# A transformer block on one core: the loops over the attention heads are replaced by instructions written out for every head

## The reference

```
q, k, v = x @ wq.T, x @ wk.T, x @ wv.T      # per head, [1024, 128]
q, k = rope(rmsnorm(q)), rope(rmsnorm(k))
s = 50 * tanh(q @ k.T * scale / 50)         # causal
x = layernorm(x + softmax(s) @ v @ wo.T)
x = layernorm(x + moe(x) + shared_ffn(x))   # 32 experts, 6 of them per token
```

## Time and profile before

| | us |
|---|---|
| median of 3 runs | 1119.45 |
| lowest, highest | 1116.04, 1123.36 |
| the profiled execution | 1122.51 |
| its span, first to last instruction | 1120.8 |
| PE busy in the span | 1038.1 |
| DVE busy | 831.9 |
| ACT busy | 699.9 |
| POOL busy | 631.6 |

### The profile page before, as it was taken

The page is one execution under the profiler, slowest core; times in us unless marked ns, Lnnn a source line. Parts: engine busy times, 40 slices in busy tenths (PEclk is TensorE's granted clock), DMA queues, the critical chain, the costliest instruction groups (busy, mean ns, idle before and its releaser), DMA issues.

```text
span 1120.8 us, 20581 instructions
## 1 busy us (share of the span) xinstructions
PE 1038.1 (93%) x6304; PEld 831.9 (74%) x6304; DVE 831.9 (74%) x1360; ACT 699.9 (62%) x1159; POOL 631.6 (56%) x668
## 2 busy tenths in 40 slices
PE   4688999999999999999999999999999959989766
PEld 3567888888888888888888888888888746445432
DVE  3377888888888888888888898988898775713203
ACT  3465777777777777777777777777777632322212
POOL 0265666666666666666666666666666652363332
PEclk9899999999999999999999999999999887989977
DMA  9100000000011010101000000000000009539427
GB/s 331 31 29 30 29 29 28 28 28 28 28 33 40 30 38 20 37 24 33 25 32 28 28 28 28 28 28 28 28 28 20 20 3 294 138 96 268 74 29 229
DMA packets 47195, 65.99 MB, mean 59 GB/s; under 512 B 7904, under 2 KB 38592, under 8 KB 47168
## 3 DMA queue, kind: packets, MB, share of 16 engines
q1 hardware_dynamic: 43376, 60.65, 17.6%
q0 software_dynamic: 3072, 4.46, 2.2%
q10 hardware_dynamic: 720, 0.54, 0.2%
HBM read 54.35 MB, written 11.29 MB: 59 GB/s over the span
## 4 chain that ended last, share of the span: by engine, by line
PE 78%; DMA 11%; DVE 5%; issue 2%; POOL 2%; ACT 1%; SPq 1%; ACTq 0%; POOLq 0%; DVEq 0%
PE ps L387 20%; PE ps L388 19%; PE ps L389 19%; PE ps L415 9%; DMA acc_rows<-ye,acci 7%; PE ps L421 4%; PE ps L559 2%; PE ps L603 2%; DMA qsq<-rq_rows 1%; DMA yacc<-in_x 1%; DVE prob_lo L1057 1%; POOL pacc L933 1%; PE ps L569 1%; DVE qhat_lo L1057 1%; POOL xg L1013 1%
## 5 line engine op out<-in xcount | busy, mean ns | idle before, releaser
L1057 DVE TENSOR_TENSOR prob_lo<-praw,prob_hi 128x1024 fp32r<-128x1024 f32 (+7 forms) x256 | 313.2, 1251 | 3.2 <-ACT prob_hi L718 3.2
L916 POOL TENSOR_SCALAR_AFFINE_SELECT praw<-praw 128x128 f32<-128x128 f32 x256 | 119.6, 469 | 307.0 <-ACT praw L765 288.4
L933 POOL TENSOR_TENSOR pacc<-pacc,praw 128x768 f32<-128x768 f32 (+2 forms) x192 | 241.8, 1259 | 16.6
L759 ACT ACTIVATE praw<-ps,rk 128x1024 f32<-128x1024 f32 (+7 forms) x256 | 186.0, 740 | 88.3 <-PE ps L389 78.5
L718 ACT ACTIVATE prob_hi<-praw 128x1024 fp32r<-128x1024 f32 (+7 forms) x256 | 168.0, 683 | 1.1 <-POOL praw L916 1.1
L765 ACT ACTIVATE praw<-praw 128x1024 f32<-128x1024 f32 (+7 forms) x256 | 167.4, 681 | 0.0
L387 PE MATMUL ps<-qhat_hi,kT_hi 128*128 128x512 f32 (+3 forms) x384 | 136.4, 355 | 13.4 <-DVE qhat_lo L1057 12.9
L387 PE MATMUL ps<-prob_hi,vS_hi 128*128 128x512 f32 (+3 forms) x384 | 136.1, 354 | 4.0 <-DVE prob_lo L1057 4.0
L389 PE MATMUL ps<-qhat_hi,kT_lo 128*128 128x512 f32 (+3 forms) x384 | 133.9, 349 | 0.0
L388 PE MATMUL ps<-qhat_lo,kT_hi 128*128 128x512 f32 (+3 forms) x384 | 133.9, 349 | 0.0
L388 PE MATMUL ps<-prob_lo,vS_hi 128*128 128x512 f32 (+3 forms) x384 | 133.3, 347 | 0.0
(11 more groups left out here) (155 smaller groups left out, 1961.1 us busy)
## 6 DMA issues: line engine op xcount, KB each, us to landing
qsq<-rq_rows SPq DMA_DIRECT2D x32, 512.0 KB, 3.7
wgu<-in_wgu SPq DMA_DIRECT2D x16, 704.0 KB
wd<-in_wd SPq DMA_DIRECT2D x16, 352.0 KB
wraw<-in_wqkv SPq DMA_DIRECT2D x16, 256.0 KB, 3.7
acc_rows<-pacc SPq DMA_DIRECT2D x8, 512.0 KB, 10.9
wv<-in_wqkv SPq DMA_DIRECT2D x16, 128.0 KB, 2.1
woraw<-in_wo SPq DMA_DIRECT2D x16, 128.0 KB, 2.0
yacc<-in_x SPq DMA_DIRECT2D x1, 2048.0 KB, 14.0
```

The costliest lines, as they stand in the source:

```text
L759: nc.scalar.activation(praw[:, raw_at(b, j)], buf[:, P * j:T], ACT.Tanh, scale=rk[:, b, j:j + 1]).then_inc(tanh_done, 1)
L916: nc.gpsimd.affine_select(out=diag, in_=diag, compare_op=ALU.is_ge, fill=0.0, base=0, pattern=[[1, P]], channel_multiplier=-1).then_inc(ma ...
L933: nc.gpsimd.tensor_tensor(pacc[:, P * j:T], before, raw, ALU.add).then_inc(pacc_done, 1)
L1057: v.tensor_tensor(dst, x_, hi.bitcast(F32), ALU.subtract).then_inc(done, 1)
```

## The change

The five hardware loops become Python loops over the same bodies. The order of the instructions of each engine stays; h is now a plain number, so that the counts waited for and the DRAM addresses are constants in the instructions, and the register instructions and the branches have nothing left to do. The bodies stand 14 times (SP: 15 times) in the program instead of once.

```
-            with sp.Fori(0, H - 1) as h:
+            for h in range(0, H - 1):
...
-            with pe.Fori(1, H - 1) as h:
+            for h in range(1, H - 1):
                 for b in range(B):
                     step(Head(h, "middle"), b)
...
-            with act.Fori(1, H - 1) as h:
+            for h in range(1, H - 1):
...
-            with pool.Fori(1, H - 1) as h:
+            for h in range(1, H - 1):
...
-            with dve.Fori(1, H - 1) as h:
+            for h in range(1, H - 1):
```

## The result

The kernel after takes 1128.27 us in the median of 20 runs (1119.78 to 1137.96), the kernel before, beside it, 1121.36 us (20 runs, 1116.04 to 1128.55). The ratio is 1.0055 with a 95% interval of 1.0031 to 1.0079: half a per cent slower, within the 1% that the prediction called no change, and 7 us where it forecast 4. Two of the 20 runs (1136.71 and 1137.96 us), over 1.5% above the fastest, count as slow and are left out of the ratio; the median of the other 18 is 1127.1 us.

The account below looks back on a forecast made before the run. The prediction took PE's own matmul stream to bound the loop. Gain 0, direct stalls 0 and collisions 5 x about 1 us, rounded down to +4, gave 1119.45 + 4 = 1123 us (+0.3%), range 1114 to 1134 us.

Parts of the forecast that it names:

- Gain of the removed instructions: Register instructions and branches in the loops: covered by PE's queued work or other engines' idle time, so worth 0.
- the upper bound: PE's 210 register instructions waiting for `values` (6.7 us) plus 14 branches (3.0 us): at most 9.7 us if uncovered.
- Step 30 of before: Already written out with constants, yet its sums came 53.92 us after step 28's, the loop's round: evidence for 0 gain.
- Packets: Instruction fetches after the change: about 51 packets on q8 and some 43 on q14, spread over the span.
- Direct stalls: Engines waiting for their own instruction fetches: taken as 0; other end of the range 37 x 1.6 = 59 us.
- Place of the collision: A fetch starting in the 3.7 us between issue and landing of the query norms' broadcast can delay it.
- the 1.2 us: Delay of the query norms' broadcast per collision with a 16 KB packet, from 5.1 - 3.9 us.
- The slow step of before: Step with the broadcast at 87 us, landing in 5.1 us, the only one of three shown beside a q8 packet.
- Number of collisions: 16 KB fetches meeting the broadcast: 14% of 37, so 5; the 8 KB packets were given 0.
- the 1.3 us of slack: Time between qhat_lo's late end and PE's use of it; said to absorb 8 KB packets' 0.6 us nearly everywhere.
- Price of one: DVE's splits pushed beside POOL's accumulation: 1.8 us with output weights, 0 to 1 us without, mean about 1 us.
- the first rival: Slower: each of 5 collisions costs PE a whole late start of 5.2 us, +26 us, 1145 us; chance 0.17.

Follow-up runs that it names:

- regs_stream: Kernel before with loops and register waits kept, but as 2 rounds of 7 heads (SP 3 of 5), so bodies are long; median 1126.96 us, ratio 1.0065.
- pe_only: Kernel after with the loops of SP, ACT, POOL and DVE put back, so only PE's loop is written out; median 1123.35 us, ratio to before 1.0033.
- others_only: Kernel before with SP, ACT, POOL and DVE written out and PE's loop kept; median 1123.69 us, ratio 1.0042.
- four_delays_light: four_delays with POOL's accumulation cut to 16 columns per tile after step 0; one run, 1107.85 us.
- after_again: The kernel after, unchanged, run once more for a second profile; one run, 1122.08 us.
- four_delays: Kernel before with SP alone written out and one more small waited-for write by SP in steps 9, 14, 19 and 24; one run, 1136.45 us.

## Why the prediction held, point by point

**Gain of the removed instructions: 0, as predicted.** Between 100 and 860 us no register instruction and no branch is left on PE, and a step without a slow trip takes the 26.96 us it took in the loop. Here are SP's loop line (L335) and PE's wait of `values` (L448), the latter beside the 210 ALU_OP of the earlier trace rows, first before:

```profile
L335 SPq FUSED_REGOPS  x15: 41/41/50, 33.5 to 793.3; - x15
L335 SPq ALU_OP  x15: 37/37/37, 87.7 to 847.0; - x15
L335 SPq COMPARE_BRANCH  x15: 40/45/50, 87.8 to 847.1; - x15
...
L448 PEldq FUSED_REGOPS  x14: 55/60/60, 95.3 to 799.4; - x14
L448 PEldq EVENT_SEMAPHORE  x4: 51/51/51, 55.0 to 898.3; - x4
```

In after L335 has no instruction, and L448 has this alone:

```profile
L448 PEldq EVENT_SEMAPHORE  x32: 51/51/51, 53.7 to 902.7; - x32
```

So in before the steps written out waited with one semaphore instruction each, and those of the loop with register instructions. Over all engines, after has 2522 ALU_OP, 497 FUSED_REGOPS, 52 MOVE and 71 COMPARE_BRANCH fewer and 560 EVENT_SEMAPHORE more, which is the whole difference of 20581 and 17999. On PE's sequencer 906 of those that went stood between 100 and 860 us and took 32.6 us together, more than the 9.7 us that the prediction took for the upper bound from two kinds of them; no step got shorter by any of it. SP issues wraw 0.39 us after the broadcast instead of 0.87. Step 30 of before had told the 0, and regs_stream, as slow with its registers, does not speak against it.

**Packets: right.** 50 on q8 and 41 on q14, where 51 and 43 were worked out. From 161 to 860 us it is 36 and 28, where before had none. That q8 is PE's shows in pe_only (50 there, 13 on q14) and in others_only (14 and 41). The other engines' packets are of 8 KB (0.34 MB in 41). PE's own stream ran on beside its packets (26 of 28 steps of pe_only stayed at 26.96 us); what shows in the steps is a small DMA with a packet beside it, with trips of up to 4.28 us in after instead of 2.2.

**Direct stalls: 0 for PE's straight code, as predicted.** pe_only shows it. The one branch that did hold PE up is regs_stream's, with 3.98 us on the sequencer and a 16 KB packet in that time; before's 14 branches took at most 0.25 us, with no packet from 161 to 860 us. For DVE, step 4 of others_only leaves the question open.

**Place of the collision: wrong in the main.** The step that failed is "a fetch that starts in the 3.7 us between a broadcast's issue and landing can touch it". Of after's seven long steps only 10 and 16 have it: their broadcasts landed in 4.4 us with a 16 KB packet and in 5.2 us with an 8 KB packet beside them. The median went from 3.7 to 3.8 us, the maximum from 5.1 to 5.2. What got slower in the other five is the write ahead of it, 2.2 us long, small and waited for: +0.7 to +1.0 us beside an 8 KB packet, up to +2.3 beside a 16 KB one. The prediction left this write out. The slow step of before, from which the 1.2 us were read the earlier trace rows, had such a trip too (2.91 us).

**Number of collisions: near, by luck.** 5 were forecast, by PE's packets alone; in after seven steps are long. Only three of them (10, 20 and 25, the last with an 8 KB packet as well) have a PE packet, 4.3 us together where the prediction has 5. The other four (9, 13, 16 and 24) are q14's, 2.9 us together, and to these it gave 0: "the 1.3 us of slack holds that nearly everywhere". It doesn't: others_only, with PE's loop kept, has 3.8 us of excess. This 0 is the term that was mis-sized.

**Price of one: right in its mechanism and in its mean, wrong in its form.** The prediction named POOL's accumulation and the row that would be contended, and four_delays_light shows that nearly all of it goes with the accumulation (step 9: 35.14 us with it, 27.61 with it cut). Its "about 1 us" stands against 7.6 us over seven long steps, 1.1 each. But the price isn't one number. Counted from the profiles, over steps 3 to 30: no split beside POOL, 0 to 1.0 us (step 16 of regs_stream, with its branch, apart); wo_lo, +1.4 to 1.9; qhat_lo, +1.7 to 2.4; qhat_hi and qhat_lo in a step without weights, +5.3; all four splits, +6.2 and +8.2. So the first rival ("a whole late start", 5.2 us) was not a rival: it is the upper part of the same staircase, and pe_only reaches it in both of its collisions. The 5.2 us of step 2 of before, from which it was read, are such a case: qhat_hi and qhat_lo take 2.62 and 2.71 us there. Steps of the kind without weights were priced at 0 to 1 us; step 20 is one of them and cost 2.0.

**The sum.** +4 forecast, for the median; +7 measured, 6.0 and 7.6 us of it in the loop of two profiles. The wide spread of after's runs (18 us, before 12) fits a price that jumps with a few tenths of a us, but no run of after above 1131.04 us was profiled, so this is argued and not shown.

**Open.** Why one 16 KB packet delays the trip and another that starts at the same offset doesn't: packets that began 1.79, 1.91, 2.06 and 2.37 us into it did, others at 1.84, 1.88, 1.92, 1.93, 1.99 and 2.02 us did not. The one at 2.37 us (step 25 of pe_only) began when a regular trip is over, so it can't be its own transfer that first held that trip up. What ties long trips to fetches is that they come with streaming and at the same steps; how a fetch holds a small write up was not seen. Which of the 16 DMA engines carried a fetch was not seen either: the profile counts the packets of q8 and q14 and those of the broadcast's q1 in shares of the same 16 (0.3, 0.1 and 8.9% from 161 to 860 us), and no more.

## What to carry to other kernels

This kernel's loop had no instruction packet from 161 to 860 us; written out it had 64. Before writing such a loop out, ask not only whether the engines have cover but which small, waited-for DMA in every round has none: here 7 of 28 steps were 0.3 to 2.0 us longer, five of them with a late write of the norms. A longer loop body was no way out here: regs_stream had 55 and 57 packets too, and paid 1.4 us for PE's branch back besides. A delay was priced here by what it pushed a short instruction into: look for DVE work that ends just before a long POOL instruction starts (qhat_lo at 180.64, the accumulation at 181.64), because the price jumped there, from at most 1.0 us with no split beside POOL to 5.3 with two and 8.2 with all four, and the mean of a few samples misleads. And where a written-out copy of a loop step already stands in the kernel, as step 30 did here, compare the two first.

## What the runs showed of the hardware

- Four DMAs of 1 KB and a wait that with no packet beside them take 2.2 us took up to 4.44 us with a 16 KB instruction packet in the time (6 of 17 such trips of after, after_again and pe_only were long), and 2.9 to 3.2 us with an 8 KB one, at DMA shares of 0.08 to 0.10 in the stretches shown. In step 25 of after one of the four took SP 0.98 us to issue, beside a 16 KB packet, instead of 0.29.
- In after, pe_only and four_delays, from step 3 on, each of DVE's splits of the queries and the output weights that began while one of POOL's accumulations ran ended behind it: qhat_lo (1.22 us alone, 2.70 to 3.02 in 4 cases) by 1.1 us, qhat_hi (0.68, 2.61 in 3) by 0.55, wo_lo (0.43, 1.44 to 2.37 in 5) by 0.3, wo_hi (0.38, 1.6 in 2) by 0.15. DVE's copies of `ps` (L1105) were not longer there: the 44 of after from step 3 on took 0.67 to 0.69 us each, and 0.69 alone.
- Of 14 rounds of some 704 PE instructions the last 13 ran with no packet on the instruction queues (before, 161 to 860 us). As 2 rounds of 7 heads they ran with 55 packets on q8, and PE's branch between the rounds took its sequencer 3.98 us and left PE's array idle for 1.15 us.
